# Attention's shift rows cleared by a transfer instead of GpSimd, weight splitting and the experts' first routing moved within the attention part

## The chip, the cores and the metric

One core of a Trainium2 chip runs the whole program. The metric is the device time of one execution in microseconds; lower is better. "Before" is the median of three executions.

## The reference, cut to what matters

`x` and `ctx` are 32 sequences of 128 tokens of width 128, in float32. The program computes:

```
h   = layernorm(x)
q, k, v    = split(h @ Wqkv + bqkv)             # 16 heads of width 8
_, ka, va  = split(ctx @ Wqkv_aux + bqkv_aux)
out = softmax(q k'/sqrt(8)) v * (1 - sigmoid(g)) + softmax(q ka'/sqrt(8)) va * sigmoid(g)
x   = x + tanh(g_xattn) * (out @ Wo + bo)

h   = layernorm(x)
s   = sigmoid(h @ gate_w.T);  sc = s + gate_bias
keep the 4 of 8 groups of experts with the largest sum of their best two sc,
then the 8 best of 64 experts; w = 2.5 * s / sum(s) over those 8, else 0
y   = sum over 64 experts of w_e * (silu(h @ Wg_e) * (h @ Wu_e)) @ Wd_e  + one shared expert
x   = x + tanh(g_ffn) * y
```

## The kernel before, in words

**Two parts.** The first part (functions of `attention`) works on *batches*, one sequence each (b = 0 to 31), in *blocks* of two (n = 0 to 15, `NC` = 16); the second part (functions of `experts`) on 8 chunks of 4 sequences, each against 33 pairs of experts (`NP`). Every engine has a program written out by hand; all order comes from these programs and from semaphores. In the attention part a body `g` covers 4 batches, k = 0 to 3, that is two blocks j = 0, 1 with n = 2g + j; `odd` is k mod 2. `LOOPS` is 8; `before_last` (also `left == 1`) is g = 6, blocks 12 and 13; `last` is g = 7, blocks 14 and 15.

**A batch in rounds.** A batch has 4 rounds r, or 8 units u = 2r, 2r+1. In a round TensorE does: the shifted scores of this batch (L1291, `shifted`, 8 matmuls into the two banks `wide`), the plain scores of batch b + 2 (L1272, `scores`, 4 matmuls, whose row maxima VectorE takes at L982), a small step of the chain that finishes batch b - 1 (transposes L1313 and L1319, projection L1326/L1327), the product with V (L1306, `weighted`), and in round 0 the transposed maxima (L1331, `turn_max`); in an even batch's round 0 also the V projections (L1250). ScalarE takes the exponentials of a round (L785, `exps`), which need the round's shifted scores and free the banks for the next. VectorE turns the maxima of batch b + 1 into `nmax` (L990 to L994) and copies their transpose to `nmaxT` (L999); ScalarE's queue then issues the transfer of `nmaxT` into rows 60 to 67 of the operand `stack_q` (L779, `shift_rows`). With these rows the shifted scores come out less the maximum. Before, `shift_rows(b + 1)` stands in round 0, ahead of `exps(b, 1)` in ScalarE's program.

**The operands.** q and k are split into three bf16 parts each, so that a product keeps float32 accuracy. For block n + 3, in block n: ScalarE copies q and k out of the bank at the odd batch's round 1 (L759, `copy_qk`), VectorE copies the auxiliary k at the odd batch's u = 5 (L1003), GpSimd makes the parts (`split`, L606 to L613; 4 instructions for q, then 2 x 4 for k; `lo_ok` counts them). SyncE stores the q parts (L401/L402) and the k parts (L408/L409) to DRAM and loads them back, rearranged, to one of three pairs of buffers `stack_q`, `stack_k` (L421 and L430, `load_stack_q`, `load_stack_k`, two transfers each). SyncE's order in block n is:

```
load_x(n+4); load_stack_q(n+2); store_k(n+2); expert_weights (L471, L474);
load_stack_k(n+2); store_x2(n-1); store_q(n+3)
```

The scores of block n + 2 start in block n + 1. Rows 64 to 67 of `stack_q`, which hold shift rows, must be zero again for the plain scores of the block that next uses the buffer: before, GpSimd does that, once a batch (`clear_shift`, L628), and TensorE waits for it (L1268).

**GpSimd's order in block n before:** clear the rows of the previous odd batch; add the bias to the residual (L635); `rest_of`: the low part of each pair of expert weights whose high part ScalarE wrote in this block (`high_of`, L808; L683 waits for `cv_hi`); clear the rows of this block's even batch, for which its shifted scores must be done; the norm's root for block n + 4 (L584 to L590); the splits of block n + 3. From block 2 to 12 `SPLIT_AT` has one pair's high part in round 0 of either batch. The norm of block n + 4 (L792) stands in the odd batch's round 2.

**The experts' first chunk.** Its statistics, norm, transposes, logits and routing are done inside the last blocks: statistics (L1030, `first_stats`) and root (L676) in block 13, norm (L817), transposes (L1344), operands (L823, L826, L1044) and logits (L1351) in block 14, routing (`first_route`, parts 0 to 13, L1054 to L1138) on VectorE in block 15, with tiles in the score banks, then the transposed weights (L1359, L836), which SyncE stores to DRAM (L549) and loads back, broadcast over partitions, as `cwb` (L557). GpSimd's first product of the experts (L1616) waits for `cwb`. An expert pair is nine 512-column matmuls (L1913 to L1915).

**The start.** The two first batches' scores are made ahead of the first body, four rounds each (L1384 and L1389), two halves of heads f = 0, 1 by two heads e = 0, 1; VectorE takes a half's maxima when both its e are there.

## Time and profile before

| | us |
|---|---|
| median of 3 executions (902.18 to 909.3) | 902.82 |
| the profiled execution's own time | 906.06 |
| its span, first to last instruction | 904.3 |
| TensorE busy, of the span | 843.3 (93%) |
| VectorE / ScalarE / GpSimd busy | 681.6 / 561.7 / 643.0 |
| mean granted TensorE clock | 0.990 |

Attention runs to about 325.7 us of the span, the experts from there to its end. The table's share of 93% is a mean over both. Where a row begins with a stretch A:B, behind it stand its length, then busy time (and instructions) of TensorE's matmuls, TensorE's weight loads, VectorE, ScalarE and GpSimd, the granted TensorE clock as a share of full speed, the DMA engines' busy share and GB/s. In the rows below a time without a unit is in us, `xN` counts instructions, and what stands in brackets is the engine's idle time before the instruction with what released it.

### The profile page before, as it was taken

The numbers are of one execution on the slowest core, as the hardware profiler recorded it, in microseconds if no ns is written. First come the engines' busy times: TensorE is split into PE (matmuls) and PEld (weight loads), VectorE is DVE, ScalarE is ACT, GpSimd is POOL, SyncE is SP. The second block draws the span as 40 slices with busy tenths as digits, with TensorE's granted clock in tenths as the row PEclk, the third lists the DMA queues.
The fourth block names the chain that finished last, engine by engine and source line by source line (L and its number), as shares of the span: only waits on it lengthen the run. The fifth ranks groups of instructions, "written<-read, shape, count | busy, mean of one in ns | idle before, by whom it ended". The sixth has DMA issues, their size and how long they took to land.

```text
span 904.3 us, 20102 instructions
## 1 busy us (share of the span) xinstructions
PE 843.3 (93%) x6765; PEld 641.6 (71%) x6765; DVE 681.6 (75%) x1652; ACT 561.7 (62%) x963; POOL 643.0 (71%) x605
## 2 busy tenths in 40 slices
PE   5789889899898879999999999999999999999997
PEld 3356656566565557888888888887888888888885
DVE  6778778688788847867866976976787786786665
ACT  4277767677777837557557557555656655655554
POOL 2466786688686227887777786777777677777775
PEclk9999999899999989999999999999999999999999
DMA  5566666756864044654745654744654655455552
GB/s 135 167 174 165 164 187 163 179 145 155 205 161 119 10 113 118 146 137 105 175 119 130 144 146 109 172 119 120 151 138 115 151 128 144 114 154 121 137 138 66
DMA packets 113619, 125.24 MB, mean 138 GB/s; under 512 B 27936, under 2 KB 75936, under 8 KB 112080
## 3 DMA queue, kind: packets, MB, share of 16 engines
q1 hardware_dynamic: 110640, 123.43, 55.0%
q8 instruction: 49, 0.80, 0.4%
q10 hardware_dynamic: 2880, 0.59, 0.3%
q14 instruction: 50, 0.41, 0.2%
HBM read 103.52 MB, written 19.96 MB: 137 GB/s over the span
## 4 chain that ended last, share of the span: by engine, by line
PE 66%; DMA 6%; DVE 3%; POOL 3%; issue 2%; ACT 2%; SPq 1%; ACTq 1%; POOLq 0%; DVEq 0%
PE bank L1913 19%; PE bank L1915 19%; PE bank L1914 19%; DMA stack_k<-k_scratch 3%; PE bank L1306 2%; PE bank L1291 1%; DMA stack_q<-nmaxT 1%; POOL hid L1616 1%; PE bank L1250 1%; ACT prob L785 1%; PE bank L1272 1%; DMA k_scratch<-parts_k 1%; PE bank L1890 1%; DVE hlo L1835 1%; DMA cwb<-wts_scratch 1%
## 5 line engine op out<-in xcount | busy, mean ns | idle before, releaser
L1616 POOL TENSOR_TENSOR hid<-act,cwb 128x512 f32<-128x512 f32 x264 | 429.1, 1634 | 141.4 <-DVE act L1831 88.1
L1665 ACT ACTIVATE silu<-bank 128x512 f32<-128x512 f32 x264 | 157.5, 597 | 204.5 <-PE bank L1915 201.4
L1831 DVE TENSOR_TENSOR act<-silu,bank 128x512 f32<-128x512 f32 x264 | 180.4, 683 | 137.6 <-ACT silu L1665 130.8
L1913 PE MATMUL bank<-xhi,weights_hi 128*128 128x512 f32 x528 | 209.6, 397 | 0.0
L1915 PE MATMUL bank<-xlo,weights_hi 128*128 128x512 f32 x528 | 207.3, 393 | 0.0
L1835 DVE TENSOR_TENSOR hlo<-hid,hhi 128x512 fp32r<-128x512 f32 x264 | 203.3, 770 | 5.2 <-ACT hhi L1670 5.1
L1914 PE MATMUL bank<-xhi,weights_lo 128*128 128x512 f32 x528 | 207.0, 392 | 0.0
L982 DVE TENSOR_REDUCE mx<-bank 128x4 f32<-128x512 f32 x256 | 165.0, 687 | 41.5 <-PE bank L1272 38.5
L785 ACT ACTIVATE prob<-bank 128x1024 f32<-128x1024 f32 x128 | 131.0, 1024 | 69.0 <-PE bank L1291 67.4
L1670 ACT ACTIVATE hhi<-hid 128x512 fp32r<-128x512 f32 x264 | 164.8, 624 | 11.9 <-POOL hid L1616 11.3
L1915 PEld LDWEIGHTS bank<-xlo,weights_hi 128*128 128x128 f32 x528 | 99.1, 188 | 22.3
L1913 PEld LDWEIGHTS bank<-xhi,weights_hi 128*128 128x128 f32 x528 | 99.1, 188 | 21.4 <-issue 0.4
L1914 PEld LDWEIGHTS bank<-xhi,weights_lo 128*128 128x128 f32 x528 | 99.3, 188 | 20.6
L1913 PE MATMUL bank<-hhi,weights_hi 128*128 128x512 f32 x264 | 104.2, 395 | 3.1 <-DVE hlo L1835 3.0
L1914 PE MATMUL bank<-hhi,weights_lo 128*128 128x512 f32 x264 | 103.3, 391 | 0.0
L1915 PE MATMUL bank<-hlo,weights_hi 128*128 128x512 f32 x264 | 103.1, 390 | 0.0
L1306 PE MATMUL bank<-prob,V 128*32 128x128 f32 x2048 | 84.4, 284 | 0.5 <-issue 0.5
L1272 PE MATMUL bank<-stack_k,stack_q 48*128 48x256 bf16 (+1 forms) x512 | 56.0, 282 | 17.7 <-DMA stack_k<-k_scratch 11.8
L683 POOL TENSOR_TENSOR weights_lo<-weights_raw,weights_hi 128x384 fp32r<-128x384 f32 x33 | 32.9, 999 | 51.5 <-ACT weights_hi L808 51.5
L1291 PE MATMUL bank<-stack_q,stack_k 64*128 64x128 bf16 (+1 forms) x1024 | 51.9, 222 | 14.7 <-ACT prob L785 12.7
L1306 PEld LDWEIGHTS bank<-prob,V 128*32 128x32 f32 x2048 | 49.4, 111 | 22.4 <-issue 17.6
L1913 PEld LDWEIGHTS bank<-hhi,weights_hi 128*128 128x128 f32 x264 | 49.5, 187 | 16.3 <-issue 2.7
(227 smaller groups left out, 970.7 us busy)
## 6 DMA issues: line engine op xcount, KB each, us to landing
cwb<-wts_scratch SPq DMA_DIRECT2D x176, 384.0 KB, 5.4
stack_k<-k_scratch SPq DMA_DIRECT2D x30, 384.0 KB
k_scratch<-parts_k SPq DMA_DIRECT2D x15, 384.0 KB, 3.3
stack_q<-q_scratch SPq DMA_DIRECT2D x30, 192.0 KB
k_scratch<-parts_k SPq DMA_DIRECT2D x15, 256.0 KB, 4.1
q_scratch<-parts_q SPq DMA_DIRECT2D x15, 192.0 KB, 2.1
xin<-in_x_dram SPq DMA_DIRECT2D x16, 128.0 KB, 2.4
cin<-in_ctx_dram SPq DMA_DIRECT2D x16, 128.0 KB, 3.2
```

The source lines that it names most:

```text
L785: act.activation(prob[pair % RP][:].rearrange("p u k -> p (u k)"), wide[:], ACT.Exp, scale=scale).then_inc(p_ok, 1)
L982: nc.vector.tensor_reduce(mx[par][:, 2 * f:2 * f + 2, 2 * r:2 * r + 2].rearrange("p a h -> p h a"), s_bank[f].rearrange("p (h a k) -> p h ...
L1272: ins = nc.tensor.matmul(s_bank[f][:, e * TC:(e + 1) * TC], q_of(n)[at, 2 * r + e, c, :], k_of(n)[at, 2 * r + e, c].rearrange("p a t -> p ...
L1306: ins = nc.tensor.matmul(to, V[i][:, a, par, h, :], prob[(ROUNDS * b + u // 2) % RP][:, j % 2, (2 * a + j // 2) * P:(2 * a + j // 2 + 1) * P],
L1616: pool.tensor_tensor(h_buf[k][:], a_buf[k][:], cwb[slot][:, q % GP, :], ALU.mult).then_inc(h_ok, 1)
L1665: act.activation(s_buf[k % RS][:], g_bank[k % 2][:], ACT.Silu).then_inc(s_ok, 1)
L1670: act.activation(hhi[k % RH][:], h_buf[k % RS][:], ACT.Copy).then_inc(hh_ok, 1)
L1831: nc.vector.tensor_tensor(a_buf[k % RS][:], s_buf[k % RS][:], u_bank[k % 3][:], ALU.mult).then_inc(a_ok, 1)
L1835: nc.vector.tensor_tensor(hlo[k % RH][:], h_buf[k % RS][:], hhi[k % RH][:].bitcast(F32), ALU.subtract).then_inc(hl_ok, 1)
L1913: nc.tensor.matmul(bank, w[0], mh, start=first, stop=False)
L1914: nc.tensor.matmul(bank, w[1], mh, start=False, stop=False)
L1915: return nc.tensor.matmul(bank, w[0], ml, start=False, stop=last)
```

## The change

What it does, part by part:

1. **Clearing.** `clear_shift` leaves GpSimd. SyncE issues one transfer per block (from n + 2 = 3 on) of 16 KB of zeros from a DRAM tensor `zero_d` to rows 64 to 67 of the block's `stack_q` (both batches at once), behind `load_stack_q(n + 2)`. The zeros are made at the start by a VectorE memset of `x2[0]` and stored by SyncE ahead of `store_first_q`. TensorE waits for it once a block.
2. **SyncE's order.** `store_k(n + 2)` moves from ahead of `expert_weights` to behind it.
3. **GpSimd's order.** `rest_of` moves behind `splits(n + 3)`. `SPLIT_AT` has both high parts of a block in its odd batch, rounds 0 and 3.
4. **The norm** of block n + 4 moves from block n's odd batch, round 2, to block n + 1's even batch, round 0 (after the copy of `osb`).
5. **Shift issue.** `shift_rows(b + 1)` moves from round 0 to round 1, behind the second exponential.
6. **The experts' first chunk** is done two batches sooner: load of `xld` at the end of block 11, statistics and root in block 12, norm, transposes, operands and logits in block 13, routing from block 14's first batch (u = 5) to block 15's first batch (u = 5), transposed weights in batch 31's rounds 0 and 1. Its tiles move out of the score banks and the late stack to the places of `full_q`/`full_k`, `parts_q` and `parts_k[0]`. In block 14 the V projections and their copy go one round later.
7. **The start.** The scores of batches 0 and 1 go half after half.

The diff, without context lines:

```diff
@@ -92,0 +93 @@
+    zero_d = nc.dram_tensor("zero_scratch", (4, H // 2 * CH * P), BF16, kind="Internal").ap()
@@ -174 +175 @@
-    q0_d, k0_d = v["q0_d"], v["k0_d"]
+    q0_d, k0_d, zero_d = v["q0_d"], v["k0_d"], v["zero_d"]
@@ -217,0 +219 @@
+    cw_at = m_cw.at
@@ -250,2 +252,7 @@
-    f_xn = m_late("f_xn", [P, K, P], F32)
-    f_xT = m_late("f_xT", [P, T], F32)
+    e_xn = m_late("e_xn", [P, K, P], F32)
+    e_xT = m_late("e_xT", [P, T], F32)
+    over_full = Map(nc, cw_at, cw_at + 3 * 1024)
+    f_xT = over_full("f_xT", [P, T], F32)
+    over_q = Map(nc, cw_at + 3 * 1024, cw_at + 6 * 1024)
+    over_k = Map(nc, cw_at + 6 * 1024, cw_at + 9 * 1024)
+    f_xn = over_k("f_xn", [P, K, P], F32)
@@ -274,2 +281,2 @@
-    f_sig_p = s_bank[0][:, 0:K * E]
-    f_sc_p = s_bank[0][:, K * E:K * E + 4 * GR].rearrange("p (g e) -> p g e", e=4)
+    f_sig_p = over_q("f_sigmoid", [P, K * E], F32)[:]
+    f_sc_p = over_q("f_scores", [P, GR, 4], F32)[:]
@@ -277,2 +284,2 @@
-    def spare(first, n):
-        return s_bank[1][:, first * GR:(first + n) * GR].rearrange("p (g e) -> p g e", e=n)
+    def part(name, n):
+        return over_q(name, [P, GR, n], F32)[:]
@@ -280,3 +287,4 @@
-    f_top_p, f_low_p, f_mid_b = spare(0, 2), spare(2, 2), spare(4, 2)
-    f_tb_p, f_lb_p, f_top_c, f_mid_c, f_pen_p = (spare(6 + n, 1) for n in range(5))
-    f_wsum_p = s_bank[1][:, 11 * GR:11 * GR + K]
+    f_top_p, f_low_p, f_mid_b = part("f_top_p", 2), part("f_low_p", 2), part("f_mid_b", 2)
+    f_tb_p, f_lb_p, f_top_c, f_mid_c = (part(f"f_{n}", 1) for n in ("tb_p", "lb_p", "top_c", "mid_c"))
+    f_pen_p = m_late("f_pen_p", [P, GR, 1], F32)[:]
+    f_wsum_p = m("f_wsum_p", [P, K], F32)[:]
@@ -309 +317,2 @@
-    shift, shift_zero = sem("shift_rows_loaded"), sem("shift_rows_cleared")
+    shift, shift_zero = sem("shift_rows_loaded"), [sem(f"shift_rows_cleared{i}") for i in range(NST)]
+    zeros_ok, zeros_st = sem("zeros_ready"), sem("zeros_stored")
@@ -341 +350 @@
-    SPLIT_AT = ([(n, c, 0) for n in range(SPLIT_FROM, LIGHT) for c in range(CH)]
+    SPLIT_AT = ([(n, 1, r) for n in range(SPLIT_FROM, LIGHT) for r in (0, 3)]
@@ -345 +354,2 @@
-    ROUTE_AT = {(2, 1): (0,), (2, 3): (1, 2), (2, 4): (3, 4, 5), (2, 5): (6, 7), (2, 6): (8, 9), (3, 0): (10, 11), (3, 1): (12,), (3, 2): (13,)}
+    ROUTE_AT = {(0, 5): (0,), (0, 7): (1, 2), (1, 1): (3,), (1, 3): (4,), (1, 5): (5,), (1, 7): (6, 7), (2, 1): (8, 9),
+                (2, 3): (10, 11), (2, 5): (12, 13)}
@@ -347 +357 @@
-    STATS_AT = ((2, 5), (2, 7), (3, 1))
+    STATS_AT = ((0, 5), (0, 7), (1, 1))
@@ -423,0 +434,4 @@
+        def clear_shift(n):
+
+            sp.dma_start(stack_q[n % NST][64:68].rearrange("p h c t -> p (h c t)"), zero_d).then_inc(shift_zero[n % NST], 16)
+
@@ -497,0 +512,3 @@
+        sp.wait_ge(zeros_ok, 1)
+        sp.dma_start(zero_d.rearrange("r (j t) -> (r j) t", j=4), x2[0][0:16].rearrange("p c t -> p (c t)").bitcast(BF16)
+                     ).then_inc(zeros_st, 16)
@@ -522 +539,4 @@
-                    store_k(n + 2, i)
+                    if n == 1:
+                        sp.wait_ge(zeros_st, 16)
+                    if n + 2 >= NST:
+                        clear_shift(n + 2)
@@ -528,0 +549 @@
+                    store_k(n + 2, i)
@@ -536 +557 @@
-                if g == LOOPS - 2 and j == 0:
+                if g == LOOPS - 3 and j == 1:
@@ -624,8 +644,0 @@
-        def clear_shift(b):
-            n, c = b // CH, b % CH
-            wait(pool, st_mm, UNITS * (b + 1))
-            none = zero[64:68, 0:1].unsqueeze(1).to_broadcast([4, HH, P // 2])
-            pool.tensor_tensor(q_of(n)[64:68, :, c, :].bitcast(F32), none, none,
-                               ALU.add).then_inc(shift_zero, 1)
-            wait(pool, shift_zero, b + 1)
-
@@ -692,3 +704,0 @@
-                if 0 < n and b - 1 + CH * NST < NB:
-                    pool.wait_ge(lo_ok, SPLITS * (n + 3))
-                    clear_shift(b - 1)
@@ -703 +713 @@
-                if left == 1 and j == 1:
+                if left == 1 and j == 0:
@@ -705,6 +714,0 @@
-                for q in range(weights_done(n - 1), weights_done(n)):
-                    rest_of(q)
-                if b + CH * NST < NB:
-                    pool.wait_ge(xb_ok, n + 1)
-                    wait(pool, cv_lo, weights_done(n))
-                    clear_shift(b)
@@ -712,0 +717,2 @@
+                for q in range(weights_done(n - 1), weights_done(n)):
+                    rest_of(q)
@@ -864,0 +871,2 @@
+                    if r == 0 and not odd and n > 0 and n + 3 < NC:
+                        norm(n + 3)
@@ -875 +883 @@
-                    if r == 0 and not (last and k == BODY - 1):
+                    if r == 1 and not (last and k == BODY - 1):
@@ -877,7 +885,9 @@
-                    if last and k == 0:
-                        if r < 2:
-                            first_norm(r)
-                        if r == 3:
-                            first_operand()
-                            first_xT()
-                    if last and k == 1 and r == 2:
+                    if before_last and k == 2 and r < 2:
+                        if r == 0:
+                            act.wait_ge(k_st[0], 32 * (NC // 2 - 1))
+                        first_norm(r)
+                    if before_last and k == 3 and r == 1:
+                        first_operand()
+                        act.wait_ge(lo_ok, SPLITS * NC)
+                        first_xT()
+                    if last and k == 0 and r == 0:
@@ -887 +897 @@
-                    if (odd, r) == (0, 1) and more:
+                    if (odd, r) == ((0, 2) if last else (0, 1)) and more:
@@ -897,3 +907 @@
-                    if odd and r == 2 and n + 4 < NC:
-                        norm(n + 4)
-                    if before_last and k == 3 and r == 3:
+                    if before_last and k == 2 and r == 3:
@@ -901 +909 @@
-                    if last and k == 3 and r == 3:
+                    if last and k == 3 and r == 1:
@@ -914,0 +923 @@
+        nc.vector.memset(x2[0][:], 0.0).then_inc(zeros_ok, 1)
@@ -1019,0 +1029,2 @@
+            if b == 0:
+                dve.wait_ge(zeros_st, 16)
@@ -1212 +1223 @@
-                    if last and k == 1 and u == 1:
+                    if left == 1 and k == 3 and u == 5:
@@ -1214 +1225 @@
-                    if last and k >= 2:
+                    if last:
@@ -1267,2 +1278,2 @@
-            if r == 0 and e == 0 and f == 0:
-                wait(pe, shift_zero, CH if n == NST else b - CH * NST + 1)
+            if c == 0 and r == 0 and e == 0 and f == 0 and n >= NST:
+                wait(pe, shift_zero[s], 16 * (n // NST))
@@ -1281,0 +1293,5 @@
+        def half_after_half(b, r):
+            for f in range(2):
+                for e in range(2):
+                    scores(b, r, e, f)
+
@@ -1341 +1356,0 @@
-            pe.wait_ge(v_ev, NC)
@@ -1356 +1371 @@
-            pe.wait_ge(fe_ok, 1)
+            pe.wait_ge(v_ev, NC)
@@ -1384 +1399 @@
-            round_of_scores(0, r)
+            half_after_half(0, r)
@@ -1389 +1404 @@
-            round_of_scores(1, r)
+            half_after_half(1, r)
@@ -1430 +1445 @@
-                    if (odd, r) == (0, 0) and more:
+                    if (odd, r) == ((0, 1) if last else (0, 0)) and more:
@@ -1433 +1448 @@
-                            pe.wait_ge(fg_ev, 1)
+                            pe.wait_ge(fe_ok, 1)
@@ -1439 +1454 @@
-                    if before_last and k == 3 and r == 2:
+                    if before_last and k == 2 and r == 2:
@@ -1441 +1456 @@
-                    if last and k == 0 and r == 2:
+                    if before_last and k == 3 and r == 0:
@@ -1443 +1458 @@
-                    if last and k == 1 and r == 1:
+                    if before_last and k == 3 and r == 3:
@@ -1445 +1460 @@
-                    if last and k == 3 and r == 2:
+                    if last and k == 3 and r == 0:
@@ -1456 +1471 @@
-    late_tiles = dict(xn=f_xn, xT=f_xT, wT=f_wT, stats=f_stats, mv=f_mv, var=f_var, rstd=f_rstd, mhalf=f_mhalf,
+    late_tiles = dict(xn=e_xn, xT=e_xT, wT=f_wT, stats=f_stats, mv=f_mv, var=f_var, rstd=f_rstd, mhalf=f_mhalf,
```

## Rows read from the trace of the kernel before

**Rows 1.** Busy time by stretch: blocks 1 to 12, block 11, block 14, block 15

```profile
61.15:274.92 213.77, 192.61 (x3174) 130.07 (x3168) 172.52 (x416) 155.88 (x249) 160.37 (x246) 0.98 0.67 172
240.84:257.39 16.55, 15.64 (x270) 10.64 (x264) 14.36 (x35) 13.00 (x21) 11.35 (x18) 1.00 0.67 168
291.37:307.75 16.38, 14.18 (x250) 9.19 (x246) 12.66 (x30) 13.59 (x24) 4.48 (x5) 1.00 0.05 13
307.75:325.68 17.93, 13.72 (x209) 8.91 (x209) 11.41 (x58) 11.69 (x17) 3.08 (x4) 0.81 0.12 31
```

**Rows 2.** Waits of TensorE in the attention part: total, times, longest

```profile
PE bank L1291 <- ACT prob L785: 12.7, 30, 1.1
PE bank L1272 <- DMA stack_k<-k_scratch: 11.8, 7, 2.7
PE bank L1291 <- DMA stack_q<-nmaxT: 1.5, 3, 0.6
```

**Rows 3.** Timeline of an even batch's second exponential: ScalarE, then TensorE (start, duration)

```profile
257.39 0.62 ACTq L779 DMA_DIRECT2D stack_q<-nmaxT  x1
258.12 1.02 ACT L785 ACTIVATE prob<-bank 128x1024 f32<-128x1024 f32 x1 [1.07 <-PE bank L1291]
...
259.20 0.40 PE L1291 MATMUL bank<-stack_q,stack_k 64*128 64x128 bf16 x8 [0.38 <-ACT prob L785]
```

**Rows 4.** Timeline of ScalarE where an issue stands behind an activation

```profile
300.22 0.62 ACTq L779 DMA_DIRECT2D stack_q<-nmaxT  x1
300.23 0.55 ACT L808 ACTIVATE weights_hi<-weights_raw 128x384 fp32r<-128x384 f32 x1
```

**Rows 5.** Timeline, block 11's odd batch: ScalarE's copy, then GpSimd

```profile
250.97 0.48 ACT L759 ACTIVATE full_k<-bank,bcol 128x256 f32<-128x256 f32 x1
...
249.91 1.03 POOL L628 TENSOR_TENSOR stack_q<-zero 4x512 f32<-4x512 f32 x1
...
252.54 0.62 POOL L606 TENSOR_TENSOR parts_q<-full_q,ones 128x256 bf16<-128x256 f32 x1
```

**Rows 6.** Timeline of SyncE's issues, q store to k load

```profile
255.38 0.36 SPq L401 DMA_DIRECT2D q_scratch<-parts_q  x1
...
258.61 1.56 SPq L421 DMA_DIRECT2D stack_q<-q_scratch  x2
260.90 0.36 SPq L408 DMA_DIRECT2D k_scratch<-parts_k  x1
...
261.84 0.59 SPq L471 DMA_DIRECT2D weights_raw<-in_L_ffn_We_gate_dram  x1
262.48 1.17 SPq L474 DMA_DIRECT2D weights_raw<-in_L_ffn_We_down_dram  x1
...
265.09 1.63 SPq L430 DMA_DIRECT2D stack_k<-k_scratch  x2
```

**Rows 7.** Timeline of TensorE at the start of block 13

```profile
272.44 0.47 PE L1272 MATMUL bank<-stack_k,stack_q 48*128 48x256 bf16 x4 [0.83 <-DMA stack_k<-k_scratch]
```

**Rows 8.** Chain of waits, one piece: start, length, what

```profile
212.88 6.23 DMA stack_q<-nmaxT
```

**Rows 9.** The hand-over: TensorE twice, GpSimd, and a stretch with its clock

```profile
319.52 0.69 PE L1319 MATMUL bank<-ident,att 128*128 128x128 f32 x2 [2.28 <-DVE att L1012]
336.31 0.47 PE L1913 MATMUL bank<-hhi,weights_hi 128*128 128x512 f32 x1 [2.33 <-DVE hlo L1835]
...
333.11 4.20 POOL L1616 TENSOR_TENSOR hid<-act,cwb 128x512 f32<-128x512 f32 x3 [16.55 <-DMA cwb<-wts_scratch]
...
319.00:322.00 3.00, 2.48 (x22) 1.42 (x22) 0.43 (x2) 0.38 (x1) 0.00 (x0) 0.50 0.04 12
```

**Rows 10.** Two stretches in which VectorE routes: part 0, parts 1 to 7

```profile
307.64:309.86 2.22, 1.91 (x36) 1.25 (x36) 2.19 (x4) 1.89 (x4) 0.19 (x1) 1.00 0.03 7
310.43:314.43 4.00, 3.53 (x70) 2.33 (x70) 3.72 (x30) 3.20 (x5) 1.58 (x2) 1.00 0.01 4
```

**Rows 11.** Timeline of VectorE, second round of batch 0's scores

```profile
25.53 1.29 DVE L982 TENSOR_REDUCE mx<-bank 128x4 f32<-128x512 f32 x2 [0.49 <-PE bank L1272]
```

More of the change, by code:

```diff
@@ L702, in body @@
                     pool.wait_ge(fc_ok, 3)
-                if left == 1 and j == 1:
+                if left == 1 and j == 0:
                     first_root()
+                if n + 3 < NC:
+                    splits(n + 3)
                 for q in range(weights_done(n - 1), weights_done(n)):
                     rest_of(q)
-                if b + CH * NST < NB:
-                    pool.wait_ge(xb_ok, n + 1)
-                    wait(pool, cv_lo, weights_done(n))
-                    clear_shift(b)
-                if n + 3 < NC:
-                    splits(n + 3)
         for g in range(LOOPS - 2):
```

## The prediction

> **What bounds the kernel now.** I read the views in this order: busy time by stretch, TensorE's waits, then the timelines of every engine around one block. TensorE is busy 93% of the span, but the loss sits in one part: the experts keep it busy nearly all the time, and nothing of the change reaches them behind their first few pairs. So the question is attention, and there the unit is the block of two batches. Blocks 1 to 12 take 213.77 us, 17.81 each, and hold 192.61 us of TensorE work, 16.05 each [rows 1]. An undisturbed block (11) takes 16.55 with TensorE busy 15.64 and VectorE 14.36, so VectorE has little room and TensorE sets the pace. Over all twelve the clock is 0.98: in places it falls to the lower of its two levels, 1.2 GHz, after TensorE sat idle for 2 us or more, and the work itself stretches, 16.05 against 15.64.
>
> Three causes make up the idle time: 30 waits for an exponential, 12.7 us in all; 7 waits for `stack_k`, 11.8 us, up to 2.7; and 3 for the shift rows, 1.5 us [rows 2]. The first is a matter of order: the second round's exponential starts at 258.12, behind an issue that occupies ScalarE from 257.39 to 258.01, and TensorE waits 0.38 for it [rows 3]. The second is a chain: q and k copied, split on GpSimd, stored, loaded. The k store waits for the last split and is issued at 260.90, the k load at 265.09 [rows 6], and TensorE gets the operand at 272.44, 0.83 late [rows 7].
>
> The third place is the hand-over. TensorE waits 2.28 us in the last batch, because VectorE is routing; the clock then stands at 0.50 [rows 9] and is 0.81 over the last 17.93 us [rows 1], which makes 6.8 us at the lower level; and the experts' fifth pair waits 2.33 us for a hidden product, as GpSimd had sat 16.55 us until `cwb` came [rows 9].
>
> **Part by part.** *The shift issue (5).* Behind an activation the issue runs beside the next one: 300.22 against 300.23 [rows 4]. So the exponential starts some 0.5 us sooner, and the issue hardly later than before. It removes 0.38 a batch where nothing else binds, 0.8 a block: 16.55 becomes 15.8. The bounds are 0 (VectorE, at 14.36 of 15.8, takes the place) and the full 12.7 us.
>
> *GpSimd's order and the clearing (1, 3).* In block 11 the q split starts at 252.54, though q and k were copied by 251.45; the 1.03 us clearing at 249.91 and the root behind it fill the time [rows 5]. Without the clearing the root is done before the copy, which itself comes some 0.35 sooner: the q split starts at 251.1 to 251.5, 1.0 to 1.4 us sooner, and so do all twelve instructions (8.3 us). The low parts of weights, 1.0 us each, then follow in GpSimd's slack (11.35 busy of 16.55 [rows 1]), so they cost nothing; the experts need them much later. SyncE pays about 0.5 us for one more issue; nobody waits for the zeros, which have most of a block to land.
>
> *The k store behind the weights (2).* SyncE reaches it later than the split ends. Worked in the frame of block 12's rows: q split from 251.1 to 253.9; q store to q load 2.4 to 3.2 us (3.23 in [rows 6]; 2.4 is my lower bound, as an estimate), take 2.9, so the q load is issued at 256.8 and takes 1.56; zeros 0.5; weights 0.59 + 1.17; k store at 260.6, against 260.90. Then 4.2 us to the k load (265.09 less 260.90), so 264.8, and up to 7.35 us for the load (272.44 less 265.09): 272.2. With no weights queued between store and load the last term may be 0.3 to 0.6 less: about 271.7. TensorE wanted it at 271.6 before (272.44 less 0.83), and with three gaps of 0.38 gone at 270.45. So about 1.2 us are missing every two blocks: (2 x 15.8 + 1.2) / 2 = 16.4 a block. The end points are 15.8 (operand in time) and 17.8 (no gain). Twelve blocks: 213.77 - 12 x 16.4 = **17.0 us** gained (0 to 24). This holds the clock too, since waits of 2 us and more, which stood ahead of each fall, go.
>
> The row shows how little of this order is certain: store and weights are issued 261 to 264, and the load's issue at 265.09 tells only when the store was complete, with the weights behind it [rows 6]. The Trainium skill ("DMA: Bandwidth & Descriptors", section "Queues, rings and completion order") says that each DMA engine consumes the descriptors of one ring in order and takes turns between the rings of different issuers. By it the k store, now behind 480 KB of weights on SyncE's queue, would pay for them, while the shift rows on ScalarE's queue would not stand behind them; that speaks against this part, and is the second rival below. No row here separates the two.
>
> *The norm (4).* It goes to a place with 0.87 us of room before the second exponential, where a weight's high part of 0.5 stood; TensorE needs it two rounds later. Nothing, 0 to 0.2 a block.
>
> *The first chunk sooner (6).* Block 13 gets the norm and the operands that block 14 had; I take 16.2 for it against 16.45: 0.2 gained. Block 14 gets parts 0 to 7 of the routing, 2.2 + 4.0 us of VectorE [rows 10], and loses the 0.7 of `first_lo`: 12.66 + 6.2 - 0.7 = 18.2 of VectorE work against 16.38 now [rows 1], so VectorE becomes the bound and the block **loses 1.8 us** (0 to 3). Block 15 is freed: the 2.28 wait goes, and the 6.8 us at the lower level (0.19 x 17.93 / 0.5) give back between 0 and 3.4; I take 2.5, as small matmuls won't gain all of it; less 0.3 for the transposes: **4.5 gained** (2 to 5.4). The transposed weights come some 6 us before the end instead of 1.4, so `cwb`, which came at 333.11, is there when the first `act` is; the 2.33 wait goes, and one of 0.9 behind it: **3.2** (2 to 3.3).
>
> *The start (7).* Batch 0's rounds have 0.5 us of idle VectorE between them [rows 11], three times; half after half fills it. Its maxima lead to the shift rows that the first batch waits for: **1.3** (0 to 2). The memset and the store of zeros lie in SyncE's and VectorE's first waits.
>
> **Sum.** 17.0 + 0.2 - 1.8 + 4.5 + 3.2 + 1.3 = 24.4 us. The profiled execution's own time is 906.06 (span 904.3 plus 1.8 around it), so 881.7; it lies 3.2 above the median of 902.82, so I forecast **878.4 us**.
>
> **The rivals.**
> - *The operand is in time* (chance 0.13): blocks at 15.8. For: the k load then has no weights beside it. Against: the 1.2 above, and VectorE at 91%. 12 x 0.6 = 7.2 more: 871.
> - *The k store pays for the weights* (0.19). For: they now stand ahead of it on the same queue. Against: the queue was nearly idle in the 2 us ahead. If the store is 2.2 us later, a block is 17.5: 13.2 us less gained, 891.6.
> - *Routing costs what it saves* (0.08): block 14's two score banks are freed later and VectorE's maxima run behind into block 15. Then 1.8 becomes 5, and of 4.5 only 1 stays: 6.7 less, 885. With it goes the case that the hand-over doesn't change at all.
> - *The shift rows come late in every batch; slower* (0.05). Place: TensorE's L1291 at a batch's start. The issue starts 2.55 us into a batch and the next begins at 7.9, so 5.3 us are left where 5.7 were; one transfer took 6.23 [rows 8]. Only 3 of the batches waited before, against it. If every one took L, a block would be 2 x (2.55 + L). The other terms give back 7.4 us, 0.6 a block, so it decides from a block of 18.4, L = 6.65. At L = 7.2 a block is 19.5: +20.3 - 7.4, so 916.
>
> **How the numbers follow.** The forecast has 0.55, with its own range of 872 to 885. About 1% (9 us) is what a measurement of this kernel can tell from no change: 893.8 is the border. The forecast, the first and third rival and most of the second lie below it: faster 0.87; the rest of the second, 0.09, within; slower 0.04. The range of eight in ten: 868 to 893.
>
> **What would show it.** Blocks 1 to 12 near 197 us; TensorE's waits for `prob` well under 5 us; `stack_k` waits down to single ones around 1 us and no stretch with a clock of 0.50 around 166; GpSimd's first split right behind L759; block 14 longer than 17 with TensorE waiting for `mx`; no 2 us wait for `att`; `cwb` no releaser. Wrong if `stack_k` waits stay at 2 us, if waits for `nmaxT` grow past 5 us in total, or if the hand-over keeps its waits.

## The result, and the profile after

| | before | after |
|---|---|---|
| median of 20 executions each, on one chip | 904.25 | 910.31 |
| the profiled execution: its time / span | 906.06 / 904.3 | 910.34 / 908.5 |
| TensorE / VectorE / GpSimd busy | 843.3 / 681.6 / 643.0 | 850.6 / 677.4 / 617.1 |
| mean granted TensorE clock | 0.990 | 0.983 |

The ratio is 1.0059 (0.0059 slower), with a 95% interval of 1.0039 to 1.008. I had forecast 878.4 us and put 0.87 on faster by over 1%. The time is within 1% of before, and what lies in the interval lies on the slow side.

The busy time by stretch of the kernel after, cut at the same events as before (the issue of the shift rows in an even batch, now L785): blocks 1 to 12, block 13, block 14, and block 15 to 0.6 us before the experts' first matmul.

```profile
61.41:282.81 221.40, 197.93 (x3172) 135.50 (x3168) 171.91 (x426) 159.77 (x252) 137.16 (x226) 0.95 0.68 166
282.81:298.61 15.80, 15.01 (x262) 9.85 (x259) 13.64 (x31) 13.23 (x23) 5.62 (x7) 0.99 0.47 130
298.61:318.16 19.55, 16.23 (x250) 9.97 (x249) 17.20 (x61) 12.04 (x20) 4.67 (x5) 0.91 0.04 10
318.16:329.00 10.84, 9.96 (x184) 6.53 (x184) 5.88 (x26) 9.77 (x14) 3.01 (x3) 1.00 0.19 53
```

Against [rows 1]: blocks 1 to 12 take 7.6 us more (213.77 before) where I had 17.0 less. TensorE executes the same instructions, busy 5.3 us longer at a clock of 0.95 instead of 0.98, and stands idle for the rest. GpSimd has 23 us less to do (160.37 before), and none of that reached the end. Block 14 takes 3.2 us more. The first expert matmul, at 325.68 before, starts at 329.64: from block 15's start to it are 11.5 us, where there were 17.9. So attention ends 4.0 us later, and the experts behind it are unchanged (578.6 and 578.9 us from their first matmul to the span's end).

TensorE's waits in the attention part (total, times, longest), after:

```profile
PE bank L1283 <- DMA stack_k<-k_scratch: 21.6, 10, 4.0
PE bank L1307 <- DMA stack_q<-nmaxT: 3.9, 5, 1.7
PE bank L1283 <- DMA stack_k<-first_k_scratch: 2.0, 1, 2.0
PE bank L1307 <- ACT prob L791: 0.8, 3, 0.4
```

The waits for an exponential went as foreseen, 12.7 us down to 0.8 [rows 2]. The waits for `stack_k` grew by nearly as much, 11.8 to 21.6 us, and these are long ones, up to 4.0. Behind five of the eight in blocks 1 to 12 the clock stands at 0.50, for 3.2 to 6.6 us each. The worst of them, from its beginning. First GpSimd's last instruction of a k split, then SyncE's issues:

```profile
115.67 0.67 POOL L634 TENSOR_TENSOR parts_k<-rest,parts_k 128x256 bf16<-128x256 f32 x1
116.30 1.00 POOL L696 TENSOR_TENSOR weights_lo<-weights_raw,weights_hi 128x384 fp32r<-128x384 f32 x1
```

```profile
113.23 1.56 SPq L431 DMA_DIRECT2D stack_q<-q_scratch  x2
114.83 0.46 SPq L436 DMA_DIRECT2D stack_q<-zero_scratch  x1
115.35 0.38 SPq L485 DMA_DIRECT2D weights_raw<-in_L_ffn_We_gate_dram  x1
115.77 0.82 SPq L488 DMA_DIRECT2D weights_raw<-in_L_ffn_We_down_dram  x1
116.64 0.60 SPq L418 DMA_DIRECT2D k_scratch<-parts_k  x1
117.28 1.50 SPq L419 DMA_DIRECT2D k_scratch<-parts_k  x1
124.47 1.56 SPq L444 DMA_DIRECT2D stack_k<-k_scratch  x2
```

And TensorE, which wants the operand, with the stretches around it (clock third from the right):

```profile
132.05 0.47 PE L1283 MATMUL bank<-stack_k,stack_q 48*128 48x256 bf16 x4 [3.97 <-DMA stack_k<-k_scratch]
```

```profile
129.00:132.00 3.00, 0.00 (x0) 0.00 (x0) 0.00 (x0) 0.14 (x1) 2.76 (x5) 1.00 0.87 214
132.00:135.00 3.00, 2.95 (x29) 2.39 (x29) 1.29 (x2) 1.36 (x3) 2.92 (x4) 0.66 0.40 107
```

The load of k can be issued only when its store has landed. That took 7.83 us here (116.64 to 124.47), where [rows 6] had 4.19. SyncE's own waits, after, say the same in sum: `L69` are the waits for a store to land, the others those for GpSimd.

```profile
SPq L69 <- DMA k_scratch<-parts_k: 55.9, 13, 5.6
SPq L411 <- POOL parts_q L634: 37.2, 14, 4.9
SPq L69 <- DMA q_scratch<-parts_q: 24.5, 13, 5.3
SPq L418 <- POOL parts_k L634: 4.5, 1, 4.5
```

SyncE waits long for GpSimd's k split once, ahead of block 1. In the thirteen blocks from 60 us on, the split had ended 0.3 to 3.5 us before SyncE came to the store. I took the chain apart over these blocks (means from the timelines of the engines, from issue to issue):

| us, mean | before | after | e1 |
|---|---|---|---|
| end of `copy_qk` to first q split | 0.94 | 0.08 | 0.08 |
| end of the last k split to the k store's issue | 0.15 | 2.00 | 0.37 |
| k store to k load (store landed) | 4.53 | 5.87 | 4.48 |
| q store to q load | 3.14 | 3.81 | 3.14 |

The chain won 0.9 us on GpSimd and lost 1.85 + 1.34 = 3.2 us on SyncE.

### The profile page after: what moved, and what is told of

Its sections match the earlier page's. It is cut to its first block, busy times and chain, and to the rows that moved or that the text cites. A ratio compares the mean times of both kernels' runs of the same rounds, so it can differ in the third digit from the quotient of the medians.

```text
span 908.5 us, 20053 instructions
## 1 busy us (share of the span) xinstructions
PE 850.6 (94%) x6765; PEld 647.7 (71%) x6765; DVE 677.4 (75%) x1653; ACT 563.5 (62%) x963; POOL 617.1 (68%) x579
## 4 chain that ended last, share of the span: by engine, by line
PE 70%; DMA 14%; POOL 4%; SPq 4%; DVE 3%; issue 3%; ACT 1%; POOLq 0%; ACTq 0%; DVEq 0%
PE bank L1928 18%; PE bank L1930 18%; PE bank L1929 18%; DMA stack_k<-k_scratch 6%; PE bank L1322 3%; DMA k_scratch<-parts_k 3%; PE bank L1307 2%; PE bank L1261 2%; DMA stack_q<-nmaxT 2%; PE bank L1283 2%; DMA q_scratch<-parts_q 1%; POOL hid L1631 1%; PE bank L1249 1%; SPq L431 1%; PE bank L1905 1%
## 5 line engine op out<-in xcount | busy, mean ns | idle before, releaser
L1850 DVE TENSOR_TENSOR hlo<-hid,hhi 128x512 fp32r<-128x512 f32 x264 | 200.8, 761 | 2.7 <-ACT hhi L1685 2.5
L1283 PE MATMUL bank<-stack_k,stack_q 48*128 48x256 bf16 (+1 forms) x512 | 60.3, 290 | 28.0 <-DMA stack_k<-k_scratch 21.6
L1930 PEld LDWEIGHTS bank<-hlo,weights_hi 128*128 128x128 f32 x264 | 49.7, 188 | 11.4
L1929 PEld LDWEIGHTS bank<-hhi,weights_lo 128*128 128x128 f32 x264 | 49.7, 188 | 11.2
```

Of the source, the lines that this page charges most:

```text
L1283: ins = nc.tensor.matmul(s_bank[f][:, e * TC:(e + 1) * TC], q_of(n)[at, 2 * r + e, c, :], k_of(n)[at, 2 * r + e, c].rearrange("p a t -> p ...
L1850: nc.vector.tensor_tensor(hlo[k % RH][:], h_buf[k % RS][:], hhi[k % RH][:].bitcast(F32), ALU.subtract).then_inc(hl_ok, 1)
L1929: nc.tensor.matmul(bank, w[1], mh, start=False, stop=False)
L1930: return nc.tensor.matmul(bank, w[0], ml, start=False, stop=last)
```

## The experiments

Theory W at the start: part 2 (the k store behind the weights) costs all that the rest of the change gains. Rivals: the loss comes from the first chunk's work, or from the shift rows.

**e1, the k store ahead of the weights.** All of the change but part 2.

```diff
@@ on_sp, after @@
                     load_stack_q(n + 2)
...
                     if n + 2 >= NST:
                         clear_shift(n + 2)
+                    store_k(n + 2, i)
                 if g < LOOPS - 2:
                     expert_weights(g, j)
...
                 if not last:
-                    store_k(n + 2, i)
                     load_stack_k(n + 2)
```

> The changed kernel with its second part undone alone: the k store goes ahead of the expert weights again (behind the transfer of zeros). Theory W (the k store pays for the 480 KB of weights queued ahead of it): from the k store's issue to the k load's issue 4.2 to 5.3 us again instead of 5.3 to 7.8, TensorE's waits for stack_k fall from 21.6 us to under 12, blocks 1 to 12 from 221.4 us to 203 to 209, the kernel to 893 to 898. Rival S (the whole chain of transfers is simply the bound once TensorE runs faster, in whatever order they are queued): blocks 1 to 12 stay within 3 us of 221, the kernel at 907 to 911.

Measured: 891.66 us, ratio to before 0.9894 (0.9851 to 0.9937). Against the change's 1.0059 one moved line is worth 1.6%, some 15 us. In e1's trace, blocks 1 to 12, 13 and 14 by stretch, TensorE's wait, and SyncE's issues of the block shown above:

```profile
62.87:265.00 202.13, 191.66 (x3172) 131.19 (x3168) 171.46 (x426) 158.89 (x251) 132.21 (x218) 0.97 0.69 180
265.00:280.87 15.87, 14.96 (x262) 9.82 (x259) 13.64 (x31) 13.52 (x25) 9.70 (x12) 1.00 0.46 129
280.87:300.56 19.69, 16.41 (x250) 10.16 (x250) 17.15 (x60) 11.95 (x20) 4.69 (x5) 0.91 0.04 10
```

```profile
PE bank L1283 <- DMA stack_k<-k_scratch: 10.7, 5, 3.3
```

```profile
117.92 0.38 SPq L418 DMA_DIRECT2D k_scratch<-parts_k  x1
118.35 0.48 SPq L419 DMA_DIRECT2D k_scratch<-parts_k  x1
118.87 0.68 SPq L485 DMA_DIRECT2D weights_raw<-in_L_ffn_We_gate_dram  x1
119.60 1.27 SPq L488 DMA_DIRECT2D weights_raw<-in_L_ffn_We_down_dram  x1
123.30 1.61 SPq L444 DMA_DIRECT2D stack_k<-k_scratch  x2
```

Store, weights, load: the load follows the store by 5.38 us here and by 4.48 in the mean, as before the change (4.53). Blocks 1 to 12 give back 19.3 us in this profile, and 15.1 in that of e9, the same kernel run again; blocks 13 and 14 stay as they were.

**e3, the same line alone.** The kernel before, with only part 2.

```diff
@@ on_sp, before @@
                     load_stack_q(n + 2)
-                    store_k(n + 2, i)
                 if g < LOOPS - 2:
...
                 if not last:
+                    store_k(n + 2, i)
                     load_stack_k(n + 2)
```

> The kernel before with only the k store moved behind the expert weights. Theory W: k store to k load grows by 1.5 to 3 us, stack_k waits from 11.8 to 25 us or more, the kernel slower by 8 to 20 us (912 to 924). Rival S: the waits stay near 12 us and the time within 3 us of before.

Measured: 918.39 us, ratio 1.0187 (1.0151 to 1.0224). k store to k load is 6.10 us in the mean (4.53 before), and the store stands 1.42 us behind the split (0.15 before). The waits for `stack_k` are 21.2 us in 9, up to 5.2, less than the 25 that I expected:

```profile
PE bank L1272 <- DMA stack_k<-k_scratch: 21.2, 9, 5.2
```

Part 2 alone costs 1.9% of the kernel before, and undoing it gives 1.6% of the kernel after. It is the cause by both tests.

**e5, the weights last of all.** If weights ahead of the store hurt, weights behind the load should be best of all, I thought.

```diff
@@ on_sp, e1 @@
+                if not last:
+                    load_stack_k(n + 2)
                 if g < LOOPS - 2:
                     expert_weights(g, j)
...
-                if not last:
-                    load_stack_k(n + 2)
```

> As e1_store_first, with the expert weights issued behind the k load too. Theory W (every transfer of the chain pays for what was queued ahead of it on SyncE's queue): the k load, which still had 480 KB of weights ahead of it, lands about 1 us sooner, the waits for stack_k fall from 10.7 to under 6 us, blocks 1 to 12 from 202.1 to 195 to 199, the kernel 3 to 6 us below e1_store_first. Rival: the q store, which now stands behind the weights instead, pays for them (q store to q load grows from 3.1 to over 4.5 us), and nothing is gained.

Measured: 911.31 us, ratio 1.0076 (1.0051 to 1.0101), 1.8% above e1's. My expectation fell. The rival that it named has the outcome right, nothing is gained, but not the place: the q store's landing grows less than it said (4.23 us to the q load, not over 4.5), and most of TensorE's waiting is for the shift rows, which it did not name. The waits between 40 and 300 us, and SyncE around one burst:

```profile
PE bank L1307 <- DMA stack_q<-nmaxT: 19.5, 10, 3.0
PE bank L1283 <- DMA stack_k<-k_scratch: 7.9, 4, 2.4
```

```profile
179.69 1.56 SPq L444 DMA_DIRECT2D stack_k<-k_scratch  x2
181.29 0.52 SPq L485 DMA_DIRECT2D weights_raw<-in_L_ffn_We_up_dram  x1
181.85 0.66 SPq L488 DMA_DIRECT2D weights_raw<-in_L_ffn_We_down_dram  x1
182.55 0.71 SPq L501 DMA_DIRECT2D x_scratch<-x  x1
183.87 0.50 SPq L411 DMA_DIRECT2D q_scratch<-parts_q  x1
184.41 2.84 SPq L412 DMA_DIRECT2D q_scratch<-parts_q  x1
```

The k load and the weights now stand next to each other. What comes up in their wake pays: the 16 KB of shift rows, which come from ScalarE's queue (19.5 us of waits, 3.4 to 3.9 in e1 and after), and the q store (3.14 us to the q load in e1). The k store, with no weights near it, is 4.44 us from the k load, as with the weights right behind it (4.48 in e1): behind the store they cost it nothing that shows. The weights have to stand somewhere, and between k store and k load they hide in a wait that SyncE has anyway.

**e6, the weights on another queue.** Is it the place in SyncE's queue, or the bytes in flight? The order of after, but ScalarE issues the weights in an even batch's rounds 0 and 1.

```diff
@@ on_sp, after @@
-                if g < LOOPS - 2:
-                    expert_weights(g, j)
...
@@ on_act, after @@
+                    if not odd and r < 2 and (g < LOOPS - 2 or g == LOOPS - 2 and k == 0):
+                        expert_part(act, g, k // CH, r)
...
                     if r == 1 and not (last and k == BODY - 1):
                         shift_rows(b + 1)
```

> The changed kernel with its weights issued from ScalarE's queue (even batch, rounds 0 and 1) instead of SyncE's, so about as early, but not in front of the k store on the same queue. Theory W1 (what costs is the order within one queue): k store to k load falls from 5.8 us in the mean to under 4.8, and the kernel comes to 885 to 898. Theory W2 (what costs is that the same 16 DMA engines are busy with the weights when the k store comes): k store to k load stays at 5.3 to 6 us, shift rows pay too, and the kernel stays above 900.

Measured: 906.84 us, ratio 1.0027 (1.0008 to 1.0045). k store to k load is 5.91 us in the mean, as in after (5.87), though nothing of the weights is in SyncE's queue; the store's issue now stands 0.38 us behind the split. So W2 holds: a store that comes behind the weights takes 1.3 to 1.6 us longer than before's 4.53 (e3, after, e6), whichever queue carries them. TensorE's waits here:

```profile
PE bank L1324 <- DMA stack_q<-nmaxT: 17.0, 15, 2.2
PE bank L1300 <- DMA stack_k<-k_scratch: 7.3, 5, 2.0
```

TensorE waits for the shift rows, now behind the weights on the same queue, 15 times, but each time no longer than in e5, where they had a queue of their own. Its waits for `stack_k` are down to 7.3 us, below e1's. Whether the sooner issue of the store did that is not shown: a TensorE that is held up at the shift rows also wants k later.

**e4, the shift issue alone.** The kernel before, with only part 5.

```diff
@@ on_act, before @@
-                    if r == 0 and not (last and k == BODY - 1):
+                    if r == 1 and not (last and k == BODY - 1):
                         shift_rows(b + 1)
```

> The kernel before with only the shift rows' issue moved behind the second exponential. My prediction's term: TensorE's waits for prob fall from 12.7 to under 2 us; where the operand chain binds part of it comes back as waits for stack_k, so the kernel gains 3 to 8 us (896 to 901). Rival: all of it comes back as waits for stack_k and the shift rows, and the time stays within 2 us of before.

Measured: 900.79 us, ratio 0.9987 (0.9956 to 1.0018): no difference that can be told. Its waits between 40 and 300 us:

```profile
PE bank L1291 <- ACT prob L785: 4.4, 10, 0.7
PE bank L1272 <- DMA stack_k<-k_scratch: 8.2, 7, 1.9
PE bank L1291 <- DMA stack_q<-nmaxT: 4.1, 4, 1.3
```

Of 11.8 us of waits for exponentials in this stretch 7.4 go (I had expected under 2 to be left), and 3.2 come back at the shift rows (0.9 before). None come back at `stack_k` (8.2, and 11.8 before), as the rival had it. In this profile blocks 1 to 12 are even 5.5 us shorter than before (208.27); its execution, 897.43 us, is below the median. So the timed executions show no gain where the profile shows one; what took it there stays open, and the interval leaves room for up to 4 us.

**e7, all but parts 2 and 5.** e1 with the shift issue in round 0 again (the diff of e4, backwards).

> As e1_store_first with part 5 undone (shift rows' issue ahead of the second exponential again). My prediction's term (0.38 a batch where nothing else binds): waits for prob back at 10 to 12 us, blocks of 15.8 back at 16.5, the kernel 5 to 9 us slower than e1_store_first (897 to 901). Rival (the operand chain binds anyway, as the null result of that part alone in the kernel before says): within 2 us of e1_store_first.

Measured: 899.43 us, ratio 0.9942 (0.9922 to 0.9962), against 0.9894 and 0.9866 for e1's kernel. The waits for `prob` are back at 13.1 us. So part 5, worth nothing that shows by itself, is worth 0.5 to 0.8% with the rest of the change beside it (e7's interval lies clear of e9's and overlaps e1's a little). Which of the other parts makes the difference was not tried.

**e8, all but parts 2 and 6.** The first chunk of the experts where it was before.

```diff
@@ on_pe, as an instance; the tiles' places too are those of before @@
-                    if before_last and k == 3 and r == 0:
+                    if last and k == 0 and r == 2:
                         first_turn_x()
-                    if before_last and k == 3 and r == 3:
+                    if last and k == 1 and r == 1:
                         first_logits()
-                    if last and k == 3 and r == 0:
+                    if last and k == 3 and r == 2:
                         first_turn_w()
@@ on_dve @@
-                    if last:
+                    if last and k >= 2:
                         for part in ROUTE_AT.get((k, u), ()):
                             first_route(part)
```

> As e1_store_first with part 6 undone (the experts' first chunk where it was before). If part 6 is worth what the stage sums of the changed kernel say (block 13 +0.65, block 14 -3.2, block 15 +6.4): 3.5 to 4.5 us slower than e1_store_first, 895 to 897. Rival: block 14's overload gives it all back, no difference beyond 1.5 us.

Measured: 896.45 us, ratio 0.9911 (0.9882 to 0.9941), against 0.9894 and 0.9866 for e1's kernel: part 6 looks worth 1.5 to 4 us, but the intervals overlap (e1's holds e8's ratio), so even its sign is not certain. Blocks 13 and 14 in its trace:

```profile
264.01:280.72 16.71, 14.51 (x259) 9.40 (x255) 14.44 (x40) 12.52 (x21) 10.56 (x15) 1.00 0.46 123
280.72:296.59 15.87, 14.47 (x254) 9.40 (x250) 12.96 (x31) 13.44 (x25) 4.49 (x5) 1.00 0.05 13
```

Block 14 takes 15.87 us with the chunk's old order and 19.69 in e1.

**e2 and e11, routing placed otherwise.** Both on e1, to win back block 14.

```diff
@@ on_dve, e1 @@
-    ROUTE_AT = {(0, 5): (0,), (0, 7): (1, 2), (1, 1): (3,), (1, 3): (4,), (1, 5): (5,), (1, 7): (6, 7), (2, 1): (8, 9),
-                (2, 3): (10, 11), (2, 5): (12, 13)}
+    ROUTE_AT = {(1, 7): (0,), (2, 1): (1, 2), (2, 2): (3, 4), (2, 3): (5, 6), (2, 4): (7, 8), (2, 5): (9, 10),
+                (2, 6): (11,), (2, 7): (12, 13)}
```

> As the run before, and the first chunk's routing moved out of block 14's batches: part 0 behind the last maxima of batch 29, parts 1 to 13 in batch 30, transposed weights one round later. Theory R (block 14 lost 3.2 us because VectorE had maxima and routing together): block 14 falls from 19.55 to 16 to 16.7 us, block 15 grows by at most 1.5, the kernel 1.5 to 3 us below the run before. Rival: what block 14 gives back comes again as TensorE's wait for att in batch 30 or 31, so no difference beyond 1 us.

e11 has part 0 at (0, 7) instead of (1, 7):

> e9 with the routing spread otherwise: part 0 alone in block 14 (its second batch-half, k = 0, u = 7), parts 1 to 13 in block 15's first batch, transposed weights one round later. e2 had part 0 in batch 29 and lost at the nmax wait of 2.8 us what block 14 had gained (2.0). Theory C (VectorE's work in block 14 is what the 19.7 us come from, and part 0's place made e2's wait): block 14 near 17.5, no nmax wait over 1.5 us, block 15 no longer than in e9 by more than 0.5: 1.5 to 2.5 us less in all, ratio about 0.987. Rival D (the routing is VectorE work of the same size wherever it stands, and block 15 has no room for it): block 15 longer by what block 14 gains, difference within 1 us.

Measured: e2 892.31 us, ratio 0.9898 (0.9861 to 0.9936), no gain on e1; e11 900.06 us, 0.9948 (0.9925 to 0.997). e2's block 14 is 2.0 us shorter (17.67, not the 16 to 16.7 of theory R), but both have one wait of over 2.5 us for `nmax`. In e2:

```profile
295.38 0.22 PE L1347 MATMUL bank<-ident_bf,nmax 128*128 128x128 bf16 x1 [2.82 <-DVE nmax L1003]
```

```profile
291.92 0.99 DVE L1065 TENSOR_SCALAR f_sigmoid<-f_sig 128x256 f32<-128x256 f32 x1
292.94 1.75 DVE L1067 RECIPROCAL f_sigmoid<-f_sigmoid 128x256 f32<-128x256 f32 x1
294.61 0.17 DVE L999 TENSOR_SCALAR bank<-mx 128x32 f32<-128x32 f32 x1
```

Part 0 is 2.7 us in one piece. At u = 7 of either batch it stands right ahead of the next batch's `nmax`, and in e2 the clock is 0.50 from 297 to 306. So e11's theory C falls: it took a later place as the cause, and it is any place right ahead of `nmax`. The change has part 0 at u = 5, but parts 1 and 2, and parts 6 and 7, at u = 7 of the two batches, 1.1 us of VectorE right ahead of `nmax` each (306.32 and 315.83), and TensorE waits 1.0 and 1.1. Rival D falls too, since e11 is 0.8% slower than e9 on the same chip. Its profiled execution, with a span of 893.2 against 894.4, doesn't hold this loss, so where it lies stays open.

**e9 and e10, e1 again and the zeros behind the store.** e9 is e1's kernel. e10 moves the transfer of zeros:

```diff
@@ on_sp, e1 @@
-                    if n + 2 >= NST:
-                        clear_shift(n + 2)
                     store_k(n + 2, i)
+                    if n + 2 >= NST:
+                        clear_shift(n + 2)
```

> The kernel of e1 (all of the change, but the k store ahead of the expert weights, behind the zeros), as the anchor for the two beside it, on one chip. Theory W (the k store pays for the 480 KB of weights issued ahead of it): 0.9894 of before was measured; 0.985 to 0.994 expected again, k store to k load 4.5 us in the mean. Rival (that ratio was the chip's or chance, and the order is worth less): 0.995 or more.

> e9 with the 16 KB of zeros issued behind the k store instead of ahead of it (part 1's place alone). Theory A (an issue ahead of the store on SyncE costs its 0.5 us, because the k chain has no slack left, and a small transfer costs nothing else): k store 0.3 to 0.5 us sooner, stack_k waits of 10.7 us down to 6 or less, 2 to 4 us less in all, ratio about 0.986. Rival B (the store waits for the last split in any case, so that the zeros are hidden ahead of it): no difference within 1.5 us, stack_k waits unchanged.

Measured, on one chip: e9 892.95 us, ratio 0.9866 (0.9839 to 0.9893); e10 896.06 us, 0.9904 (0.9878 to 0.9931). e9 confirms e1. In e10 the store stands 0.04 us behind the split (0.37 in e1) and the waits for `stack_k` fall to 6.0 us, those for the shift rows rise to 6.9. Its profiled execution, with a span of 886.4, was the shortest of all (e9's 894.4), and its median is no better: theory A, right by this one profile, falls by the timed executions. Rival B doesn't hold either, since it had the waits unchanged and the times within 1.5 us. The two intervals just overlap, so whether e10 is slower is not told.

e1's kernel is the best that was run: 1.1 to 1.3% ahead of before, and by the ratios 1.6 to 1.9% ahead of after.

## Why the prediction was wrong

*Blocks 1 to 12, +17.0 forecast, -7.6 measured.* The steps in order:

- The exponentials: right. The waits are gone, and the issue costs ScalarE nothing. That this is worth 0.8 us a block, 9.6 in twelve, was too simple: alone it gave nothing that shows (e4), and with the rest of the change 4 to 7 us (e7).
- GpSimd's order: right. The q split starts 0.08 us behind the copy in nearly every block (1.12 before), and the low parts behind the splits hinder nobody.
- **The k store behind the weights: this step failed, in two terms.** The smaller one is SyncE's path to the store. By my numbers the last split ends at 259.4 (251.1 + 8.3) and the store comes at 260.6, 1.2 us behind it. Measured are 2.00 in the mean, up to 3.5. The issues from q load to k store were sized right (3.8 us against 3.68); the landing of the q store was not: I took 2.9 us to the q load, and it is 3.81 in the mean, up to 6.3. The larger one is the k store's own landing. I carried "then 4.2 us to the k load" over from a row in which the weights stood behind the store. With them ahead it is 5.87 in the mean and up to 7.8. The rows had no case of it; I had listed it as the second rival with 2.2 us and 0.19, and took the value of the nearest row for the forecast. Against before the two are 1.85 + 1.34 = 3.2 us.
- The rival's price was the other error. I gave it 13.2 us. Measured are 15 to 17 us (e1, e3, e9). From e1 to after TensorE's waits for `stack_k` grow by 10.9 us, and its busy time in blocks 1 to 12 by 6.3 (191.66 to 197.93), as the clock is at 0.50 there for some 23 us and not 10. I had counted the lateness and left out the clock.

What I expected of the k load "with no weights between store and load", 0.3 to 0.6 us off, agrees with the rows: where TensorE waited for the operand, it came 7.70 us behind the load's issue in the mean of six waits before, 7.37 in eight after and 7.10 in eight in e3. It is small against the 3.2.

Part 2 is not the whole miss. Blocks 1 to 12 fell short by 24.6 us (17.0 forecast, 7.6 lost), and it accounts for 15 to 17. With the store ahead, e1 reaches 202.1 us for these blocks (e9 206.3, e10 199.0) and not 196.8: 7.5 to 15 us gained instead of 17.0. The forecast had 1.2 us missing every two blocks, 7 in all; e1 and e9 still wait 10.7 and 10.6 us for `stack_k`. The unit of 16.4 us is reached where the chain is in time: e1's blocks 6 to 12 take 16.3 each (150.86 to 265.00), its first five 17.6, with `stack_k` waits of 3.3 and 2.4 us and the clock at 0.50 behind both.

*Block 13, +0.2.* Measured +0.65: the right sign, for a term too small to matter.

*Block 14, -1.8.* Measured -3.2. VectorE's work is 17.20, under my 18.2, so the sum of work was on the safe side, but the block takes 19.55. TensorE waits only 3.3 us in all (twice 1.0 and 1.1 for `nmax`), and the clock is 0.50 in the stretch behind the first of them:

```profile
307.60:310.60 3.00, 2.11 (x29) 1.36 (x33) 2.96 (x11) 1.67 (x3) 0.99 (x1) 0.97 0.07 20
310.60:313.60 3.00, 3.00 (x42) 1.47 (x33) 2.93 (x11) 1.41 (x2) 0.00 (x0) 0.50 0.04 8
```

The clock that I gave back in block 15 was in part taken in block 14. The term left that out.

*Block 15, +4.5.* Measured +6.45, above the 5.4 that I had as its bound. From 318.16 to 329.64 TensorE is busy 10.60 us (13.72 before) and idle 0.9 (4.2). The stretch at 0.50 went, and the 6.8 us at the lower level gave back nearly all that they could, where I took 2.5 of 3.4; of the idle time 2.4 us are waits for `att`, as forecast, and the rest smaller waits that I had not counted.

*`cwb`, +3.2.* Wrong: 0.3. The wait stays.

```profile
336.74 4.20 POOL L1631 TENSOR_TENSOR hid<-act,cwb 128x512 f32<-128x512 f32 x3 [10.60 <-DMA cwb<-wts_scratch]
```

```profile
339.95 0.47 PE L1928 MATMUL bank<-hhi,weights_hi 128*128 128x512 f32 x1 [2.01 <-DVE hlo L1850]
```

The transposed weights are copied at 325.85, 3.8 us before the experts' first matmul and not 6; then the store (issued at 326.46), the issue of `cwb` at 328.51, and 8.2 us until it is there. And the experts start sooner relative to it, since block 15 got shorter: the two moved together.

*The start, +1.3.* Measured -0.3. The waits for VectorE's maxima fell, from 4.8 to 3.1 us up to 61 us, but TensorE waits 2.0 us for the first k operand (0.7 before), and the `stack_k` waits of this part are 2.3 us against 1.1. That the store of zeros, which now precedes the first stores on SyncE, makes them late was not tried.

*The other rivals.* The operand in time (871) and late shift rows (916) did not come about in the change. The second has its mechanism in e5 and e6, though: 19.5 and 17.0 us of such waits, and some 1.8% and 1.3% above e1. The third is near what e8 suggests: part 6 gives 1.5 to 4 us, if anything, where my terms for it (0.2 - 1.8 + 4.5 + 3.2) gave 6.1.

Sum by stage of the measured: -0.3 - 7.6 + 0.65 - 3.2 + 6.45 - 0.2 (experts) = -4.2, the two spans' difference.

## What to carry to other kernels

In a chain of store and load through DRAM, the interval from the store's issue to the load's issue holds only for the order in which it was measured. When bulk transfers move from behind the store to ahead of it, price both the issues that now come first and the longer landing, and where the operand is already late, add what the clock loses. Bulk transfers hide best in a wait that the queue has in any case, here between the store and the load that waits for it; giving them another queue did not bring the store's landing back (e6). An edit can show nothing alone and something beside others (part 5 in e4 and e7), and one profile of a kernel is not its time (e10).

## What the runs showed of the hardware

- 480 KB of weights in flight make a store of 640 KB that is issued behind them land 1.3 to 1.6 us later, on the same queue (4.53 us before, 5.87 after, 6.10 in e3) or on another (5.91 in e6). Issued behind the store they leave it as it is (4.48 in e1, against 4.44 in e5 with no weights near). The Trainium skill ("DMA: Bandwidth & Descriptors", section "Queues, rings and completion order") says that a DMA engine takes turns between the rings of different issuers. This case does not contradict it, but the 16 KB of shift rows on ScalarE's queue still had TensorE waiting up to 3.0 us when k load and weights stood together on SyncE's (e5): taking turns was no protection for a small transfer.
- An issue itself can take several times its usual length: SyncE's issue of half a store, 0.5 us as a rule, took 1.50 at 117.28 and 2.84 at 184.41 in the rows above, both behind weights. It happens elsewhere too (1.70 at 153.23 before, with no weights ahead), and what decides it is not shown.
- TensorE, at full clock, waited 1.01 us for `nmax` at 308.18 with waits of 0.3 to 0.6 us around it (busy 3.8 us of the 6 from 304.6), and 0.50 of the clock followed, for 3 us; the same came at 290.44 in e1. I had looked for this only behind waits of 2 us and more. Nor does such a wait always bring it: behind waits of 2.37 us (at 238.36, before) and 2.19 us (at 260.18, after) the clock stayed at 1.00.
